# Attention stage: where the score maxima of later head groups stand between TensorE's other passes

## The chip, the cores and the metric

One Trainium2 chip, of which this kernel uses one core. The metric is the device time of one execution in microseconds (us), lower is better. A core has five engines that run their own instruction streams and wait for each other on semaphores: PE (TensorE, matmuls), DVE (VectorE), ACT (ScalarE), POOL (GpSimd) and SP (SyncE, here only a DMA queue). PE writes its results into eight PSUM banks, numbered 0 to 7, of 128 x 512 floats each.

## The reference

One macaron block over x of 2048 tokens by 512: half an expert layer, an attention, half an expert layer, each on a layernorm of x and added to x.

```python
x = x + 0.5 * _L0_ffn_ref(_layernorm(x), router_w, w1, w2, w3)
x = x + _L0_attn_ref(_layernorm(x), wq, wk, wv, wo)
x = x + 0.5 * _L0_ffn_ref(_layernorm(x), router_w, w1, w2, w3)
```

The attention is what the change touches. It has 16 query heads and 4 key and value heads of 32 columns, a rotary embedding on q and k, a causal mask and a softmax:

```python
attn = jnp.einsum('bhqd,bhkd->bhqk', q, k) / np.sqrt(HD)
attn = jnp.where(mask[None, None], -jnp.inf, attn)
attn = jax.nn.softmax(attn, axis=-1)
out = jnp.einsum('bhqk,bhkd->bhqd', attn, v)
return out.transpose(0, 2, 1, 3).reshape(b, t, d) @ wo
```

## The kernel before

The stages follow one another: routing and experts, the projections of q, k and v, attention, routing and experts again. All orders are written out by hand; each engine runs its own list.

In attention the work is cut into **groups** G = 0 to 15. Group G is the block b = G // 4 of 512 queries and the key head G % 4, with its four query heads. A group's **tiles** are (G, k), k = 0 to 4 b + 3, each 128 keys; the list `TILES` has 160 of them. For each tile PE makes four **scores** (L1614, one a head, keys on the partitions, 512 queries wide, fewer where the mask cuts), ACT takes exp of each (L1731, into P), POOL masks the diagonal tiles (L1770), and PE **weighs** V with them into bank 3 (L1626). Sums of P over the keys are made by PE with a matrix of ones into bank 4 (L1644) for tiles in `SUMMED`. From group 8 on, most tiles of a group are added up elsewhere instead: by POOL into CH (L1784, four additions a tile) and by DMAs that accumulate into CD (L1800), which PE sums once at the group's end (L1635). P has two buffers for groups 0 to 7, four after that.

Softmax needs a maximum over the keys for each query and head before the exp. It comes in as a bias: rows 96 and 97 of Qs hold the negative maximum (as a high and a low part) against ones in Ks, so the score already has it taken off. So for every group the maxima are made ahead of time, by a second set of products with the queries on the partitions: `pe_top` (L987) into a free bank, then `dve_top`, a reduction on DVE into a column of PM (L1000 where the mask doesn't cut, L1002 on the diagonal, which adds the mask and reduces). The page speaks of them as "bank<-Ks,Qs" and "PM<-bank". Such a maximum covers 512 keys, on the diagonal 128 to 512. `tops_of(G)` lists them: 16 times (b + 1) a group. Groups 0 to 3 get theirs during the projections, groups 4 to 15 during attention.

When a group's last maximum is through, `dve_found_in_bank` ("solvemax", L1033, L1038, L1040) brings PM together into M, PE transposes M ("found", L1049), ACT copies that to mT (L1058, "foundcopy"), and SP writes it to DRAM and reads it back into Qs (L1079, L1083). The group's first score waits for that.

`attend_plan` writes one list of steps, `g.plan`; every engine walks the same list and does the steps that are its own. For each tile n it appends four scores of tile n; after each score come the maxima that are due; after the second score one entry of `extra` (work of a finished block: its four out **projection** chunks "proj", L1681, then statistics, scaling, transposes and logits); after the fourth the weigh of tile n - 1, a solvemax ahead of it and a found behind it where one is due, and for a finished group "out", "tsum" (L1652) and "even" (L1661) at set distances. How many maxima are due follows from two counters, `weight` (work passed) and `given` (maxima put, a diagonal one by its share of 512 keys).

Maxima, projection chunks, tsum, even and found share a ring of banks, taken in turn: 5, 6 and 7, and 4 as well for a part of each group from 8 to 13. `pe_take` makes PE wait until the bank's last user, on DVE or ACT, has freed it. After the last maximum the scores get two of those banks in addition to their three (`g.wide`). PE runs its list in order, so a maximum that waits for a bank holds all that stands behind it.

Of the kernel before, what the change touches and what calls it, by code (L numbers as in the profile page):

```python
# [15 lines left out]
NB = 4  # L16
BQ = 512
# [959 lines left out]
def tops_of(G):  # L977
    return [("top", G, h, c, k) for h in range(4) for c in range(4) for k in range(G // 4 + 1)]
# [438 lines left out]
def first(b, k):  # L1417
    return max(0, k - 4 * b) * P


TILES = [(G, k) for G in range(4 * NB) for k in range(4 * (G // 4) + 4)]
# [20 lines left out]
def summed_by_pe(G):  # L1442
    others = added_by_pool(G) + added_by_dma(G) + added_by_dve(G)
    return [k for k in range(4 * (G // 4) + 4) if k not in others]


def numbered(tiles):
    return {n: i for i, n in enumerate(tiles)}
# [7 lines left out]
SUMMED = numbered(n for n, (G, k) in enumerate(TILES) if k in summed_by_pe(G))  # L1456
# [25 lines left out]
    return todo + [[("logits", b)], [("best", b)]]  # L1482


def attend_plan(g):

    ring, plan = g.ring, []
    ahead = [key for G in range(4, 4 * NB) for key in tops_of(G)]
    later = {}
    told, weight, given, extra, known, copying, free = 4, 0.0, 0.0, [], [], [], True  # L1490

    def put(at, step):
        later.setdefault(at, []).append(step)
# [7 lines left out]
    for n, (G, k) in enumerate(TILES):  # L1501
        b = G // 4
        for j in range(4):
            at = 4 * n + j
            plan.append(("score", n, j))
            weight += (BQ - first(b, k)) / BQ
            while ahead and given < 1.1 * weight:
                key = ahead.pop(0)
                given += 1 if key[4] < key[1] // 4 else (key[3] + 1) / 4
                plan.append(key)  # L1510
                if not ahead or ahead[0][1] != key[1]:
                    known.append((at + 1, key[1]))
                    told += 1
# [3 lines left out]
            if copying:  # L1517
                plan.append(("foundcopy", copying.pop()))
            if j == 1 and extra:
                plan += extra.pop(0)  # L1520
            if j == 3 and n:
                if known and known[0][0] <= at and free and n - 1 not in LAST.values():
# [5 lines left out]
                if n - 1 in LAST.values():  # L1528
# [5 lines left out]
                    if G0 % 4 == 3:  # L1534
                        if b == 1:
                            residual(at + 2, 0)
                        until = at + (34 if b == 1 else 9)
# [432 lines left out]
def build(nc, d, out):  # L1970
    ctx = ExitStack()
    with ctx:
# [11 lines left out]
        project_plan(g)  # L1984
        g.projected = {bank: g.ring.uses[bank] for bank in (5, 6, 7)}
        attend_plan(g)
        g.routed = [None, None]
        pe, act, dve, pool, sp = nc.tensor, nc.scalar, nc.vector, nc.gpsimd, nc.sync
# [118 lines left out]
```

## Time and profile before

| | |
|---|---|
| time, median of 3 runs | 1305.88 us (1305.64 to 1311.02) |
| the profiled execution, its own time | 1308.35 us |
| its span on the core | 1307.1 us |
| PE busy, share of the span | 90% |
| DVE, ACT, POOL busy | 69%, 50%, 46% |
| attention, first score to the last | 425.8 to 1029 us |
| mean granted clock of PE over the span | 0.964 |

The span is what the profiler saw on the core; the profiled execution's time has some 1.2 us around it. Busy shares are means over stages with different limits, so the attention stage has to be read by itself: by stretches of a group each, and in the timeline. Matmuls overlap in the rows (a full score lasts 0.40 us, and the next starts some 0.24 us later), so it is the distance between starts that tells what one costs. "PEld" is the load of a matmul's weights, which runs beside the matmuls and waits before they do. An instruction's row may name in brackets the idle time of its engine before it and what ended that.

### The profile page before, as it was taken

What the parts mean: (1) busy time and instruction counts of PE and PEld (TensorE: products, weight loads), DVE (VectorE), ACT (ScalarE), POOL (GpSimd) and SP (SyncE); (2) the same over time, 40 slices, a digit from 0 to 9 for tenths busy, and PEclk for the clock granted to TensorE, in tenths of its full rate; (3) what the DMA queues carried; (4) which work ended last, traced back from release to release, by engine and by line L of the source; (5) the groups of instructions that cost most, each with busy time, mean ns of one, the idle gap of its engine ahead of it and who ended that gap; (6) DMA issues with size and microseconds to landing.
All of it is one profiled execution on the core that took longest, in us unless ns stands there. A gap on an engine that the chain in (4) does not pass through costs nothing.

```text
span 1307.1 us, 21775 instructions
## 1 busy us (share of the span) xinstructions
PE 1174.8 (90%) x7252; PEld 773.6 (59%) x7252; DVE 902.5 (69%) x2104; ACT 660.1 (50%) x1313; POOL 596.7 (46%) x495
## 2 busy tenths in 40 slices
PE   4589999949998999999999999999999958999996
PEld 3468888728776555445545455445544436777774
DVE  8867777759997566476677677577754675666664
ACT  2545555426555555255456566356567733444442
POOL 4644544314110111001436556455582463888886
PEclk9789999979999899999999999999999968999999
DMA  9823333356430123014445845556733452666665
GB/s 339 337 90 114 107 112 106 121 170 108 88 69 4 33 47 55 1 38 95 98 107 153 163 98 121 171 130 158 144 88 65 136 197 52 99 106 101 101 103 72
DMA packets 66971, 146.92 MB, mean 112 GB/s; under 512 B 8784, under 2 KB 28240, under 8 KB 62864
## 3 DMA queue, kind: packets, MB, share of 16 engines
q0 software_dynamic: 35184, 93.34, 33.9%
q1 hardware_dynamic: 31680, 52.19, 11.7%
q8 instruction: 62, 1.02, 0.3%
q14 instruction: 45, 0.37, 0.1%
HBM read 79.71 MB, written 33.55 MB: 87 GB/s over the span
## 4 chain that ended last, share of the span: by engine, by line
PE 61%; DVE 16%; DMA 10%; issue 5%; ACT 3%; POOL 3%; SPq 0%; POOLq 0%; DVEq 0%; ACTq 0%
PE bank L830 10%; PE bank L1614 10%; PE bank L1626 9%; PE bank L987 8%; PE bank L853 6%; DMA out<-Y,DI 4%; PE bank L1644 4%; PE bank L1681 3%; DMA XG<-xn,TK 3%; DVE bank L1002 2%; DVE PM L1000 2%; PE bank L812 2%; POOL out L780 2%; PE bank L725 2%; PE bank L1379 2%
## 5 line engine op out<-in xcount | busy, mean ns | idle before, releaser
L1731 ACT ACTIVATE P<-bank 128x512 f32<-128x512 f32 (+3 forms) x640 | 303.4, 536 | 260.2 <-PE bank L1614 253.6
L1000 DVE TENSOR_REDUCE PM<-bank 128x1 f32<-128x512 f32 x384 | 252.6, 685 | 82.8 <-PE bank L987 82.0
L1614 PE MATMUL bank<-Qs,Ks 98*128 98x512 f32 (+3 forms) x640 | 241.1, 407 | 5.2 <-ACT P L1731 2.8
L987 PE MATMUL bank<-Ks,Qs 96*128 96x512 f32 (+3 forms) x640 | 234.2, 386 | 10.8 <-DVE PM L1002 5.4
L1614 PEld LDWEIGHTS bank<-Qs,Ks 98*128 98x128 f32 x640 | 117.2, 190 | 131.4 <-issue 59.4
L1770 POOL TENSOR_SCALAR_AFFINE_SELECT P<-P 128x512 f32<-128x512 f32 x64 | 42.7, 675 | 287.2 <-ACT P L1731 287.2
L1002 DVE CUSTOM_DVE_ANT_0 bank<-bank,KB 128x128 f32<-128x128 f32 (+3 forms) x256 | 124.6, 498 | 54.8 <-PE bank L987 54.1
L987 PEld LDWEIGHTS bank<-Ks,Qs 96*128 96x128 f32 x640 | 121.8, 191 | 56.8 <-DVE PM L1000 17.2
L1626 PE MATMUL bank<-P,V 128*32 128x512 f32 (+3 forms) x1280 | 151.5, 545 | 3.6 <-POOL P L1770 3.6
L780 POOL DMA_INDIRECT out<-Y,DI x78 | 127.6, 1636 | 41.7 <-issue 32.0
L1784 POOL TENSOR_TENSOR CH<-CH,P 128x512 f32<-128x512 f32 x108 | 139.2, 1434 | 14.1 <-ACT P L1731 13.4
L941 DVE TENSOR_TENSOR DL<-W,DH 128x512 fp32r<-128x512 f32 x152 | 98.3, 689 | 41.4 <-ACT DH L902 41.4
L757 POOL DMA_INDIRECT XG<-xn,TK x78 | 93.5, 1199 | 52.2 <-DVE TK L688 18.0
L902 ACT CAST DH<-W 128x512 fp32r x152 | 86.7, 618 | 20.9 <-issue 20.9
L830 PE MATMUL bank<-WH,XH 128*128 x312 | 94.1, 424 | 2.2 <-ACT XH L882 1.5
L830 PE MATMUL bank<-WL,XH 128*128 x312 | 87.0, 401 | 0.2 <-DVE XL L923 0.2
L830 PE MATMUL bank<-WH,XL 128*128 x312 | 85.5, 395 | 0.0
L769 POOL DMA_INDIRECT y<-Y,DI x39 | 38.7, 993 | 97.1 <-DVE Y L951 97.1
L923 DVE TENSOR_TENSOR XL<-bank,XH 128x512 fp32r<-128x512 f32 x78 | 53.9, 691 | 35.6 <-ACT XH L882 35.6
L882 ACT CAST XH<-bank 128x512 fp32r<-128x512 f32 x78 | 45.8, 587 | 58.4 <-PE bank L812 55.6
L888 ACT ACTIVATE G<-bank 128x256 f32<-128x256 f32 x78 | 29.9, 384 | 86.1 <-PE bank L830 86.1
L830 PEld LDWEIGHTS bank<-WL,XH 128*128 128x128 f32 x312 | 59.6, 191 | 15.3 <-issue 0.9
(193 smaller groups left out, 1946.9 us busy)
## 6 DMA issues: line engine op xcount, KB each, us to landing
CD<-P POOLq DMA_DIRECT2D x17, 1024.0 KB, 7.4
xn<-XN SPq DMA_DIRECT2D x8, 1024.0 KB, 5.9
WR<-L_ffn_w POOLq DMA_DIRECT2D x16, 512.0 KB, 15.1
XO<-y POOLq DMA_DIRECT2D x8, 1024.0 KB, 9.4
WR<-L_ffn_w SPq DMA_DIRECT2D x16, 512.0 KB, 7.7
CD<-P SPq DMA_DIRECT2D x7, 1024.0 KB, 5.3
CD<-CH POOLq DMA_DIRECT2D x7, 1024.0 KB, 7.5
XA<-y POOLq DMA_DIRECT2D x24, 256.0 KB, 4.2
```

The lines of the kernel that those rows point to most:

```text
L757: pool.indirect_dma_start(out=x.XG[:, j % NG, :], out_offset=None, in_=g.xnd[f][:, :], in_offset=bass.IndirectOffsetOnAxis(ap=r.TK[:, j:j ...
L780: pool.indirect_dma_start(out=g.out.rearrange("t (h d) -> (t h) d", h=2), out_offset=bass.IndirectOffsetOnAxis(ap=r.DI2[:, h, j:j + 1], ax ...
L830: ins = pe.matmul(bk(g, 2 + j % 2), part[:, k * P:k * P + P], w[:, bass.ds(ev[j] * 2048 + k * 512, 512)], start=(n == 0 and k == 0), stop= ...
L902: act.copy(x.DH[:, k, :], W.W3[:, bass.ds(e * 1024 + k * 512, 512)]).then_inc(s("dh"), 1)
L941: ins = dve.tensor_tensor(x.DL[:, k, :], W.W3[:, bass.ds(e * 1024 + k * 512, 512)], DHf[:, k, :], ALU.subtract)
L987: pe.matmul(bk(g, bank)[:, 0:n], g.Qs[b][0:96, G % 4 * 4 + h, c * P:c * P + P], g.Ks[0:96, G % 4, k * BQ:k * BQ + n], start=True, stop=Tru ...
L1000: dve.tensor_reduce(dst, bk(g, bank)[:, 0:n], AX.X, ALU.max).then_inc(s(f"free{bank}"), 1)
L1002: dve.tensor_tensor_reduce(out=bk(g, bank)[:, 0:n], in0=bk(g, bank)[:, 0:n], in1=g.KB[:, CB_MASK + BQ - n:CB_MASK + BQ], scale=1.0, scalar ...
L1614: pe.matmul(bk(g, bank)[:, o:BQ], g.Ks[0:98, G % 4, k * P:k * P + P], g.Qs[G // 4][0:98, G % 4 * 4 + j, o:BQ], start=True, stop=True).then ...
L1626: ins = pe.matmul(bk(g, 3)[32 * h:32 * h + 32, o:BQ], g.V[:, k, q * HD:q * HD + HD], a.P4[buffer_of(n)][:, h, o:BQ], start=(k == 0), stop= ...
L1731: act.activation(a.P4[buffer_of(n)][:, j, o:BQ], bk(g, score_bank(g, i))[:, o:BQ], ACT.Exp, scale=scale).then_inc(s("exp"), 1)
L1784: ins = pool.tensor_tensor(to[:, h, :], two[:, h, :], one[:, h, :], ALU.add)
```

## The change

Only `attend_plan` is touched, and two small functions that it calls are new. The pace at which maxima are put was 1.1 for each full score; the scores alone counted as passed work. Now `passes_of(n)` counts for a tile its scores, weighing and, in `SUMMED`, its sums, cut to the columns that the mask leaves, and one more; a projection chunk counts `PROJ_PASSES`. The share of maxima for each pass is set so that they come out even up to tile (14, 10), the eleventh of group 14. A projection's passes are added when its chunk is put, so its maxima come after the next score.

```diff
+PROJ_PASSES = 10
+
+def passes_of(n):
+    G, k = TILES[n]
+    return (8 + (4 if n in SUMMED else 0)) * (BQ - first(G // 4, k)) / BQ + 1
+
+def part_of(key):
+    return 1 if key[4] < key[1] // 4 else (key[3] + 1) / 4
...
+    until = TILES.index((14, 10))
+    share = sum(part_of(key) for key in ahead) / (sum(passes_of(n) for n in range(until)) + 3 * NB * PROJ_PASSES)
...
-            weight += (BQ - first(b, k)) / BQ
-            while ahead and given < 1.1 * weight:
+            weight += passes_of(n) / 4
+            while ahead and given < share * weight:
                 key = ahead.pop(0)
-                given += 1 if key[4] < key[1] // 4 else (key[3] + 1) / 4
+                given += part_of(key)
                 plan.append(key)
...
             if j == 1 and extra:
+                weight += PROJ_PASSES if extra[0][0][0] == "proj" else 0
                 plan += extra.pop(0)
```

All lines behind the new functions stand 20 lower in the new file (L1614 is L1634 there, L1626 L1646, L1644 L1664, L1681 L1701); L987 and L1049 stay.

The first place is PE at the second projection chunk of block 0, in tile (5, 3). Before, from the chunk to the weigh:

```order
L1681 MATMUL bank<-WO,OT_154 128x512 x4
L1614 MATMUL bank<-Qs_134,Ks 128x512
L987 MATMUL bank<-Ks,Qs_134 128x384
L987 MATMUL bank<-Ks,Qs_134 128x512
L1614 MATMUL bank<-Qs_134,Ks 128x512
L987 MATMUL bank<-Ks,Qs_134 128x512
L1626 MATMUL bank<-P_152,V 32x512 x4
```

And now, on PE at the same chunk:

```order
L1701 MATMUL bank<-WO,OT_154 128x512 x4
L1634 MATMUL bank<-Qs_134,Ks 128x512
L987 MATMUL bank<-Ks,Qs_134 128x256
L987 MATMUL bank<-Ks,Qs_134 128x512
L987 MATMUL bank<-Ks,Qs_134 128x384
L987 MATMUL bank<-Ks,Qs_134 128x512 x2
L987 MATMUL bank<-Ks,Qs_135 128x512
L1634 MATMUL bank<-Qs_134,Ks 128x512
L987 MATMUL bank<-Ks,Qs_135 128x512
L1646 MATMUL bank<-P_152,V 32x512 x4
```

Six maxima stand behind the chunk's score where there were two, in a ring of three banks (the second row of "x2" is the last diagonal one of a group, which is 512 wide too).

The second place is PE at find 13. Before, in tile (12, 10):

```order
L1614 MATMUL bank<-Qs_136,Ks 128x512
L987 MATMUL bank<-Ks,Qs_136 128x512
L1614 MATMUL bank<-Qs_136,Ks 128x512
L987 MATMUL bank<-Ks,Qs_136 128x128
L987 MATMUL bank<-Ks,Qs_136 128x512
L1626 MATMUL bank<-P_153,V 32x512 x4
L1049 MATMUL bank<-K,M_54 8x128 x4
```

And now, on PE in tile (12, 6):

```order
L1701 MATMUL bank<-WO,OT_154 128x512 x4
L1634 MATMUL bank<-Qs_136,Ks 128x512
L987 MATMUL bank<-Ks,Qs_136 128x512 x4
L1634 MATMUL bank<-Qs_136,Ks 128x512
L987 MATMUL bank<-Ks,Qs_136 128x512
L1646 MATMUL bank<-P_153,V 32x512 x4
L1049 MATMUL bank<-K,M_54 8x128 x4
```

The find has moved four tiles ahead, behind the last chunk of block 2 and five maxima. On DVE it stands behind the chunk's addition and the same five reductions.

## Rows read from the trace of the kernel before

**Rows 1.** The page's busy time of each engine.

```profile
PE 1174.8 (90%) x7252; PEld 773.6 (59%) x7252; DVE 902.5 (69%) x2104; ACT 660.1 (50%) x1313; POOL 596.7 (46%) x495
```

**Rows 2.** Busy time by stretch, groups 5 and 9; columns in the first line.

```profile
core 0: us, PE busy (x) PEld busy (x) DVE busy (x) ACT busy (x) POOL busy (x), PEclk, DMA share, GB/s
...
515.10:560.60 45.50, 44.52 (x269) 22.07 (x267) 24.11 (x64) 16.23 (x36) 2.54 (x4) 1.00 0.09 16
...
684.60:731.50 46.90, 43.95 (x326) 24.55 (x327) 34.03 (x91) 26.93 (x55) 26.57 (x24) 1.00 0.62 149
```

**Rows 3.** Timeline of PE, tiles (10, 6) to (10, 9) and (15, 5): start, us.

```profile
751.10 0.50 PE L1614 MATMUL bank<-Qs,Ks 98*128 98x512 f32 x1
...
754.28 0.50 PE L1614 MATMUL bank<-Qs,Ks 98*128 98x512 f32 x1
...
762.42 1.06 PE L1626 MATMUL bank<-P,V 128*32 128x512 f32 x8
...
1005.78 1.20 PE L1614 MATMUL bank<-Qs,Ks 98*128 98x512 f32 x4
...
1007.90 1.19 PE L1614 MATMUL bank<-Qs,Ks 98*128 98x512 f32 x4
```

**Rows 4.** Waits of PE, 625 to 1000 us: total, times, longest.

```profile
PE bank L1049 <- DVE M L1040: 5.8, 7, 1.6
PE bank L1626 <- POOL P L1770: 2.6, 3, 1.2
```

**Rows 5.** Waits of PE's weight loads, 625 to 1000 us.

```profile
PEld bank L987 <- DVE PM L1000: 10.6, 36, 0.4
...
PEld bank L987 <- ACT mT L1058: 2.5, 6, 0.5
...
PEld bank L1614 <- ACT mT L1058: 1.3, 1, 1.3
```

**Rows 6.** Waits of PE's weight loads, 425 to 625 us.

```profile
PEld bank L987 <- DVE PM L1000: 6.7, 21, 0.5
...
PEld bank L987 <- ACT mT L1058: 3.9, 5, 1.0
```

**Rows 7.** Busy time by stretch of 4 us, columns as in rows 2.

```profile
860.00:864.00 4.00, 2.35 (x15) 0.91 (x14) 3.67 (x11) 1.33 (x3) 4.00 (x5) 1.00 0.64 131
864.00:868.00 4.00, 3.91 (x23) 2.09 (x20) 1.96 (x9) 3.29 (x6) 2.29 (x2) 1.00 0.66 135
868.00:872.00 4.00, 2.70 (x12) 1.05 (x14) 3.85 (x13) 3.99 (x7) 0.00 (x0) 0.93 0.69 266
872.00:876.00 4.00, 4.00 (x22) 1.45 (x15) 1.56 (x3) 0.74 (x3) 1.43 (x2) 0.64 0.48 98
```

**Rows 8.** Timeline behind a projection chunk, tile (8, 3).

```profile
641.29 0.69 DVE L1833 TENSOR_TENSOR XO<-bank,XO 128x512 f32<-128x512 f32 x1 [2.26 <-PE bank L1681]
641.33 0.40 PE L987 MATMUL bank<-Ks,Qs 96*128 96x512 f32 x1
```

**Rows 9.** Timeline of maxima and a find, tiles (6, 0) and (6, 1).

```profile
558.01 0.57 DVE L1002 CUSTOM_DVE_ANT_0 bank<-bank,KB 128x384 f32<-128x384 f32 x1 [0.73 <-PE bank L987]
...
558.50 0.69 DVE L1000 TENSOR_REDUCE PM<-bank 128x1 f32<-128x512 f32 x1
...
560.31 1.27 DVE L1000 TENSOR_REDUCE PM<-bank 128x1 f32<-128x512 f32 x2
...
561.04 0.50 PE L987 MATMUL bank<-Ks,Qs 96*128 96x512 f32 x1 [0.24 <-DVE PM L1000]
...
565.20 0.16 DVE L1033 TENSOR_REDUCE bank<-PM 128x16 f32<-128x32 f32 x1
565.40 0.17 DVE L1038 CAST M<-bank 128x16 fp32r<-128x16 f32 x1
```

**Rows 10.** Timeline of POOL, tiles (10, 4) to (10, 8).

```profile
744.66 10.06 POOL L1784 TENSOR_TENSOR CH<-CH,P 128x512 f32<-128x512 f32 x8 [0.57 <-ACT P L1731]
...
755.56 5.01 POOL L1784 TENSOR_TENSOR CH<-CH,P 128x512 f32<-128x512 f32 x4
760.53 0.63 POOL L1770 TENSOR_SCALAR_AFFINE_SELECT P<-P 128x512 f32<-128x512 f32 x1
```

## The prediction

> **What bounds the kernel now.** I read the page first: PE is busy 1174.8 of 1307.1 us, DVE 902.5, POOL 596.7 [rows 1]. The change touches the attention stage alone, some 605 us of the span, so next came the busy time by stretch there: in groups 5 and 9 PE is busy 44.52 of 45.5 us and 43.95 of 46.9, at a granted clock of 1.00 [rows 2]. PE bounds the stage. A product for maxima ("a maximum" below) is PE work wherever it stands, so moving one gains nothing unless it takes a wait with it. I call a maximum over 512 keys one unit, a shorter one its share (128 keys a quarter).
>
> What a unit costs on PE comes from whole tiles in the timeline, from the first score of one to the first score of the next. Tile (10, 6) holds 4.5 units and takes 754.28 - 751.10 = 3.18 us; tile (15, 5) holds none and takes 1007.90 - 1005.78 = 2.12 [rows 3]. So a unit is (3.18 - 2.12) / 4.5 = 0.236 us, and neither tile has slack in it: at the density of before, a plain tile doesn't wait for DVE. I then looked at waits. From 625 us to 1000, PE sat idle 5.8 us in seven places before the transposes of "found" (L1049, for DVE's M) and 2.6 us for POOL's masks [rows 4]. Its weight loads, which run ahead and so wait longer than PE loses, waited 10.6 us for DVE to free the bank of a maximum and 2.5 + 1.3 us for the copy of mT on ACT [rows 5]; from 425 us to 625 the same two are 6.7 and 3.9 us [rows 6]. That is all the change can win: some 10 to 25 us of waits out of 1308.
>
> **The change, part by part.** Nothing is added or removed: 576 maxima of 504 units in all, 640 scores, 12 finds. What moves is where the maxima stand. The rate was 1.1 units a full score; it is now 504 / (1286 + 120) = 0.358 units a pass. A full tile without sums on PE counts 9 passes and gets 3.2 units instead of 4.4, one with sums counts 13 and gets 4.7, and a projection's chunk counts 10 and brings 3.6 at once. Counted over the plan, groups 0 to 4 change little (3.0 to 3.3 units a tile after 2.8, 3.9 after 3.5 in group 4), group 5 goes from 3.56 to 5.59, groups 9 to 11 and 13 from 3.8 to 3.9 down to 3.2, and the last maximum moves from (14, 7) to (14, 9).
>
> *Thinned tiles, a gain.* With 3 to 4 maxima a tile DVE keeps up. Of the 10.6 us of weight-load waits on DVE in the later stretch PE itself loses a part only; nothing shows which, so the bounds are 0 and 10.6, and I take 3.5, near the low end, because the plain tile of rows 3 has no wait and the waits sit where other DVE work (the inverse sums, statistics) comes between.
>
> *Finds, a gain.* "solvemax" stands behind the last maximum on DVE, and "found" behind one weigh on PE. In the later stretch the seven finds cost 5.8 us of idle PE [rows 4]. Six of the seven of after stand in tiles with less DVE work ahead or with a doubled weigh in front; I give them 1.2 us together. Find 13 is the exception: it moves from (12, 10) to (12, 6), right behind a projection's burst. DVE there has the projection's add and five maxima, 6 x 0.60 us, and the find's three short steps, 0.2 us apart [rows 9], 4.2 us in all, against PE's score, five maxima, score and weigh, 2.6 us: some 1.7 us of wait with the transfer of the last one. So 5.8 - 2.9 = 2.9 us gained, between 0 and 5.
>
> *The copy of mT, a gain.* A maximum that is next on the find's bank waits until ACT has copied it. With fewer maxima a tile the ring comes round later. Finds 6 and 8 to 14 no longer have a maximum on that bank within two or three scores, finds 4, 5 and 7 do. Of 3.9 + 2.5 + 1.3 us [rows 5, 6] I take 3, bounds 0 and 6.
>
> *A stretch at low clock, a gain.* From 860 to 872 us PE is busy 2.35, 3.91 and 2.70 of 4 us each, and from 872 to 876 the granted clock is 0.64 [rows 7], that is partly at the lower of its two levels, 1.2 GHz. The idle time is find 13 at (12, 10) and then a square root's table on ACT at (12, 11). The find goes from there, so the second wait stands alone, and I expect no fall: 4 us at 0.64 instead of 1.00 is 1.4 us, with the rest of a slow tile at its edges 2.0. Bounds 0 and 2.
>
> *Bursts behind projections, a loss.* Each of the 12 chunks (L1681) is followed in the new plan by a score and then 4 to 6 maxima in a row, where before stood 1 or 2. The ring has three banks in group 5, and DVE adds the chunk first. In the rows, with the first maximum at 641.33 as zero, DVE's add starts at -0.04 and lasts 0.69 [rows 8]. Two reductions in a row take 1.27 us, one of them 0.69, so the next instruction starts some 0.60 after a full one; a 384 wide one takes 0.57 and lets the next start after 0.49, and PE goes on 0.05 us after a reduction has ended (560.31 + 0.69 gives 561.00, PE 561.04) [rows 9]; for 256 columns I estimate 0.43 and 0.33 from these. At (5, 3) the row after the chunk is half, full, 3/4, full, full, full, score, full. PE starts them at 0, 0.12, 0.70 (chunk's bank, free at 0.65), 1.04, 1.63, 2.11, the score at 2.35, the last at 2.72, and ends at 2.96. Without waits it is 1.74: 1.2 us lost. Four such chunks in group 5 make 4.8; waits of 0.8 us that stood in these tiles already (they are in rows 6) come off: 4.0. With four banks (groups 8 and 12) the same working gives 0.3 to 0.5 for five in a row and 0 to 0.25 for four: 1.5 + 0.8 us for eight chunks. Together 6.3, bounds 2 (if reductions and the add overlap more than in these rows) and 9.
>
> *POOL, a loss.* POOL's additions don't get shorter when the maxima thin out. In group 10 eight of them start at 744.66 and take 10.06, four more at 755.56 take 5.01, the mask at 760.53 ends at 761.16, and PE's weigh needs it at 762.42 [rows 3, 10]. The stretch from 744.66 is 16.5 us of POOL and 17.8 of PE. PE loses 17.5 - 13.25 = 4.25 units there, 1.0 us, and the find's 0.7; it arrives after 16.1 and waits some 0.6 us. Groups 9 to 11 alike give 1.8, group 13 nearly reaches the same bound, say 0.4: 2.2 us, bounds 0 and 6. In group 14 the wait for the mask stays, since from (14, 4) POOL is the longer chain before and after.
>
> *Sum.* Gains 3.5 + 2.9 + 3.0 + 2.0 = 11.4; losses 6.3 + 2.2 = 8.5; net 2.9 us faster. The profiled execution took 1308.35 (span 1307.1), 2.5 above the median of 1305.88, so 1305.4 for it and **1303.0** for the median.
>
> **Rivals.**
> *Evenness pays in full.* If the waits for freed banks were PE's nearly whole, thinning gains 8 us instead of 3.5, mT 5 and the finds 4: 19 less 9.5, some 9.5 faster, **1296.5**. For it: the 36 waits of the later stretch sit in the very tiles that are thinned. Against it: the plain tile without slack [rows 3].
>
> *POOL takes over.* If POOL's chain from the second addition to the mask is the longer one in groups 9 to 13 more often than worked out, up to the bound of 6 us, what the thinning gives is handed to POOL: 2.9 - 3.8 = -0.9, **1306.8**. For it: 16.5 against 17.8 us, a slack of 1.3 that any gain eats. Against it: groups 8 and 12 stretch by the projections, and POOL has room there.
>
> *The bursts bring the clock down* (slower). In group 5 a burst lets PE idle 1.2 us in 2.96, four times 8 to 10 us apart, and find 13 idles 1.7 just behind another. If each of the five is followed by a stretch like 872 to 876, 2.0 us apiece, and the old fall stays, 2.9 - 10 - 2 makes 9 slower: **1312 to 1313**. [...] Against it: a tile of group 5 with 1.2 us of wait in some 9 is 87% busy, and group 9 with 2.95 us idle held 1.00 [rows 2]. The Trainium skill speaks for this rival ("TensorE: Matmul & The Clock Gate", section "A second HAM failure mode: psum-queue depth-cycling"): a kernel that cycled through PSUM banks let PE pause briefly between groups of matmuls, and its clock swung between the two levels. By that page the time would be this rival's 1312.5; the trace agrees in rows 7 and not in rows 2, so its chance stays small.
>
> **How the numbers follow.** The forecast 0.57 (1299.5 to 1307 by its bounds), evenness in full 0.21, POOL 0.13, clock 0.09. A measurement here tells about 0.5%, 6.5 us, from no change. Faster by more (below 1299.4): most of the second case and the low edge of the first, 0.24. Slower by more (above 1312.4): most of the clock's, 0.07. The rest, 0.69, is the same. For 8 in 10 the range leaves half of the second case below (0.11) and the clock's above (0.09): 1296 to 1310.
>
> **What would show it.** Right: in group 5 four gaps of some 1.2 us in maxima behind L1701, waiting for PM; groups 9 to 11 some 2 to 3 us shorter each and group 5 some 8 longer (2.03 units x 8 tiles x 0.236 = 3.8, and the waits); waits for M of some 3 us after 625 us; a granted clock of 1.00 at (12, 12); POOL's mask a little late in groups 10 and 11. Wrong: bursts without gaps, a second stretch of low clock, or thinned groups that don't shrink.

## The result and the profile after

The changed kernel takes **1319.41 us** (median of 5 runs, 1317.81 to 1323.43); the kernel before, beside it, 1306.71 (5 runs, 1305.64 to 1311.02). The ratio is **1.0093**, 95% interval 1.0069 to 1.0116: 12.7 us slower, where 1303.0 was forecast with a range of 1296 to 1310. The forecast has the wrong sign and the time lies outside the range. The profiled execution is the longest of the five, 1323.43 us with a span of 1322.2 (before 1307.1), so the places below add up to 15.1 us and not to 12.7.

The page's busy time of each engine, after, answers to [rows 1]:

```profile
PE 1182.8 (89%) x7252; PEld 774.5 (59%) x7252; DVE 907.8 (69%) x2104; ACT 657.9 (50%) x1313; POOL 597.2 (45%) x495
```

The counts are the same, as they must be. PE is 8 us longer at the same work: matmuls that ran at a lower clock, or stalled on their way. The rest is idle time.

To find the places I took the time from each group's first exp to the next group's. A unit of maxima that moves takes its 0.236 us of PE along, so the table's fifth column takes that off: what is left is what the move cost or gave.

| groups | before, us | after, us | units moved in | difference less 0.236 a unit | what the prediction had put there |
|---|---|---|---|---|---|
| 0 to 3 | 54.6 | 55.7 | 4.8 | 0.0 | 0 |
| 4 | 31.2 | 33.6 | 2.8 | +1.8 | 0 |
| 5 | 45.6 | 54.7 | 16.2 | **+5.3** | +4.0, bursts |
| 6 | 32.8 | 37.6 | 2.0 | **+4.3** | 0 |
| 7 | 34.8 | 34.5 | 2.8 | -0.9 | 0 |
| 8 | 55.6 | 60.6 | 5.8 | **+3.6** | +1.5, bursts |
| 9 to 11 | 129.5 | 119.9 | -24.5 | -3.9 | +1.8 POOL, and most of -3.5, -2.9, -3.0 |
| 12 | 73.7 | 76.0 | 2.5 | **+1.7** | +0.8 bursts, -2.0 clock |
| 13 | 58.0 | 57.5 | -11.2 | **+2.1** | +0.4 POOL |
| 14, 15 | 86.3 | 84.2 | -1.0 | -1.9 | 0 |

With +1.3 ahead of the attention and +1.8 behind it, where nothing was changed, that is the 15.1 us between the two spans. In one place the table shows this one execution more than the plan: group 9 takes 43.2 us here and 41.5 to 41.6 in the six variants below whose plan is the same there, so groups 9 to 11 gave nearer 5.5 us than 3.9.

Groups 5 and 9 in the busy time by stretch (columns as in [rows 2], the bounds by first exp):

```profile
517.07:571.75 54.68, 52.30 (x286) 25.07 (x285) 34.05 (x87) 16.77 (x35) 2.54 (x4) 1.00 0.15 37
704.44:747.67 43.23, 42.75 (x316) 23.93 (x317) 30.16 (x80) 26.36 (x57) 27.24 (x25) 0.96 0.65 158
```

Against [rows 2], PE's idle time in group 5 grew from 1.0 to 2.4 us and in group 9 it fell from 3.0 to 0.5. Note that "busy" hides part of group 5's loss: a matmul that stalls on its way is shown longer.

The waits that the prediction counted, after, answering to [rows 4 and 5] (638 to 1013 us) and, the last two, to [rows 6] (425 to 638):

```profile
PEld bank L987 <- DVE PM L1000: 3.2, 10, 0.4
...
PE bank L1634 <- ACT P L1751: 6.6, 3, 3.6
PE bank L1049 <- DVE M L1040: 4.5, 5, 1.7
```

```profile
PEld bank L987 <- DVE PM L1000: 11.6, 36, 0.7
...
PE bank L1681 <- DVE PM L1000: 2.6, 2, 2.4
```

The weight loads' waits for freed banks did fall in the thinned groups, from 10.6 us to 3.2. In the early groups they rose, from 6.7 to 11.6: there the ring has three banks and the maxima stand closer. And there are two waits that nobody had asked for: 6.6 us for P, one of them 3.6 long (before, 2.6 us in two places), and 2.4 us at L1681.

**Where the new waits stand.** The attention's first 12 us run partly at the lower clock in both kernels (0.93, 0.50 and 0.68 from 424 us before; 0.73, 0.70 and 0.50 after). From 440 us on, one stretch of 4 us before showed a clock well below 1.00 [rows 7]. After, seven do, at four places (columns as in [rows 2]):

```profile
584.00:588.00 4.00, 2.55 (x44) 1.55 (x48) 2.68 (x8) 1.97 (x3) 0.00 (x0) 0.82 0.01 4
588.00:592.00 4.00, 4.00 (x20) 1.63 (x12) 1.40 (x4) 1.63 (x3) 0.00 (x0) 0.75 0.00 0
704.00:708.00 4.00, 3.56 (x25) 1.81 (x29) 2.79 (x6) 3.04 (x8) 0.64 (x1) 0.76 0.00 2
708.00:712.00 4.00, 4.00 (x32) 2.45 (x23) 2.58 (x8) 2.76 (x5) 0.00 (x0) 0.82 0.66 262
884.00:888.00 4.00, 1.59 (x5) 1.37 (x6) 3.53 (x14) 3.67 (x7) 0.17 (x1) 0.87 0.16 33
888.00:892.00 4.00, 4.00 (x22) 1.32 (x21) 2.19 (x4) 1.07 (x2) 1.43 (x2) 0.70 0.16 33
948.00:952.00 4.00, 3.34 (x14) 1.10 (x18) 0.69 (x1) 1.75 (x4) 1.48 (x2) 0.57 0.62 127
```

Three of the four places are at a **solve**: the step in `finish_plan` in which DVE and ACT work out a finished block's layernorm scale (L294 to L318 on DVE, a square root on ACT at L338, with a load of ACT's table before it and another one back to exp). It is on neither engine's list of busy lines, since its steps are short. But both run in order, so a solve holds their lists up for some 2 us: maxima wait on DVE, exps on ACT.

*Tile (6, 2), block 0's solve.* Timelines of PE and DVE:

```profile
582.57 0.50 PE L987 MATMUL bank<-Ks,Qs 96*128 96x512 f32 x1
585.45 1.08 PE L1681 MATMUL bank<-K,R 128*32 128x128 f32 x32 [2.38 <-DVE PM L1000]
586.32 1.74 PE L1646 MATMUL bank<-P,V 128*32 128x512 f32 x8
587.77 2.00 PE L1664 MATMUL bank<-P,ones 128*32 128x512 f32 x8
```

```profile
582.84 0.17 DVE L297 TENSOR_SCALAR sm<-mv 128x4 f32<-128x4 f32 x1
583.61 0.18 DVE L310 RECIPROCAL sm<-sm 128x4 f32<-128x4 f32 x1 [0.60 <-ACT sm L338]
...
584.62 0.69 DVE L1000 TENSOR_REDUCE PM<-bank 128x1 f32<-128x512 f32 x1
```

PE stands at "even" (L1681), whose bank is held by a maximum that DVE reads only at 584.62, behind the solve. PE idles 2.38 us. Then the same weigh and sums that take 1.06 and 1.04 us elsewhere take 1.74 and 2.00: PE has been granted its lower level (1.2 GHz) for a while. In the kernel before, "even" stood in the same tile and found its bank free:

```profile
569.35 1.08 PE L1661 MATMUL bank<-K,R 128*32 128x128 f32 x32
```

*Tiles (12, 11) and (12, 12), block 2's solve.* DVE, POOL, ACT and PE:

```profile
881.29 2.91 DVE L297 TENSOR_SCALAR sm<-mv 128x4 f32<-128x4 f32 x1
```

```profile
878.94 5.22 POOL L1804 TENSOR_TENSOR CH<-CH,P 128x512 f32<-128x512 f32 x4
```

```profile
884.24 0.20 ACT L338 ACTIVATE sm<-sm 128x4 f32<-128x4 f32 x1 [2.41 <-DVE sm L297]
```

```profile
886.40 0.50 PE L1634 MATMUL bank<-Qs,Ks 98*128 98x512 f32 x1 [3.56 <-ACT P L1751]
```

An instruction on 128 x 4 numbers, 0.17 us in the solve of (6, 2), lasts 2.91 here. It ends at 884.20; POOL's run of four additions ends at 884.16. In the kernel before, the same instruction started 0.22 us behind the end of POOL's additions, and PE's wait was 1.30 us:

```profile
861.04 5.25 POOL L1784 TENSOR_TENSOR CH<-CH,P 128x512 f32<-128x512 f32 x4
```

```profile
866.51 0.17 DVE L297 TENSOR_SCALAR sm<-mv 128x4 f32<-128x4 f32 x1
```

```profile
869.68 0.50 PE L1614 MATMUL bank<-Qs,Ks 98*128 98x512 f32 x1 [1.30 <-ACT P L1731]
```

In the changed kernel ACT waits for it, with sqrt's table already loaded, the next exps wait behind that on ACT, and PE idles 3.56 us.

*Tile (13, 13).* ACT, POOL and PE:

```profile
948.11 1.76 ACT L1751 ACTIVATE P<-bank 128x384 f32<-128x384 f32 x4 [4.09 <-DMA CD<-P]
```

```profile
938.36 2.08 POOL L1820 DMA_DIRECT2D CD<-P  x1
```

```profile
948.66 0.69 PE L1634 MATMUL bank<-Qs,Ks 98*128 98x384 f32 x1 [1.82 <-ACT P L1751]
```

An exp here may overwrite P only when a transfer that POOL issues behind its additions has read it. POOL issued it at 938.36, behind the additions and a load of the residual, the exps began at 948.11, when it had landed, and PE idled 1.82 us.

The fourth place, at 704 us, is block 1's solve, with a wait of 1.18 us for P.

### The profile page after: what moved, and what is told of

It reads as the page before. It is cut to its first block, busy times and chain, and to the rows that moved or that the text cites. A ratio compares the mean times of both kernels' runs of the same rounds, so it can differ in the third digit from the quotient of the medians.

```text
span 1322.2 us, 21775 instructions
## 1 busy us (share of the span) xinstructions
PE 1182.8 (89%) x7252; PEld 774.5 (59%) x7252; DVE 907.8 (69%) x2104; ACT 657.9 (50%) x1313; POOL 597.2 (45%) x495
## 4 chain that ended last, share of the span: by engine, by line
PE 58%; DVE 17%; DMA 9%; POOL 6%; issue 6%; ACT 2%; SPq 0%; POOLq 0%; DVEq 0%; ACTq 0%
PE bank L830 10%; PE bank L1634 9%; PE bank L1646 8%; PE bank L987 8%; PE bank L853 5%; DMA out<-Y,DI 4%; PE bank L1664 4%; PE bank L1701 3%; POOL out L780 3%; DVE PM L1000 2%; DMA XG<-xn,TK 2%; DVE bank L1002 2%; POOL CH L1804 2%; PE bank L812 2%; PE bank L1379 2%
## 5 line engine op out<-in xcount | busy, mean ns | idle before, releaser
L1634 PE MATMUL bank<-Qs,Ks 98*128 98x512 f32 (+3 forms) x640 | 239.4, 408 | 8.4 <-ACT P L1751 6.6
L987 PE MATMUL bank<-Ks,Qs 96*128 96x512 f32 (+3 forms) x640 | 235.4, 390 | 10.9 <-DVE PM L1002 5.7
L1634 PEld LDWEIGHTS bank<-Qs,Ks 98*128 98x128 f32 x640 | 117.7, 191 | 137.3 <-ACT P L1751 68.3
L1646 PE MATMUL bank<-P,V 128*32 128x512 f32 (+3 forms) x1280 | 153.0, 550 | 3.5 <-POOL P L1790 3.5
L987 PEld LDWEIGHTS bank<-Ks,Qs 96*128 96x128 f32 x640 | 122.1, 192 | 56.4 <-DVE PM L1000 14.8
L1664 PE MATMUL bank<-P,ones 128*32 128x512 f32 (+3 forms) x664 | 68.3, 482 | 1.0 <-DVE PM L1000 0.5
```

Source lines behind the costliest of these rows:

```text
L987: pe.matmul(bk(g, bank)[:, 0:n], g.Qs[b][0:96, G % 4 * 4 + h, c * P:c * P + P], g.Ks[0:96, G % 4, k * BQ:k * BQ + n], start=True, stop=Tru ...
L1634: pe.matmul(bk(g, bank)[:, o:BQ], g.Ks[0:98, G % 4, k * P:k * P + P], g.Qs[G // 4][0:98, G % 4 * 4 + j, o:BQ], start=True, stop=True).then ...
L1646: ins = pe.matmul(bk(g, 3)[32 * h:32 * h + 32, o:BQ], g.V[:, k, q * HD:q * HD + HD], a.P4[buffer_of(n)][:, h, o:BQ], start=(k == 0), stop= ...
L1664: ins = pe.matmul(bk(g, 4)[32 * h:32 * h + 32, o:BQ], g.ones[:], a.P4[buffer_of(n)][:, h, o:BQ], start=fresh, stop=last)
```

## The experiments

Each edit is against the changed kernel unless another is named. The kernel before was measured beside them (medians 1306.4 to 1307.8 us), and each ratio is to that. Two questions: is the loss the bursts behind projection chunks, and is it what the moved maxima meet elsewhere?

### No counting of the chunks

```diff
-PROJ_PASSES = 10
+PROJ_PASSES = 0
```

> The changed kernel with PROJ_PASSES 0: a projection chunk brings no maxima of its own, the other passes carry them all (0.392 units a pass instead of 0.358). Theory A (bursts behind the 12 chunks cost some 7 us, and waits that collide with the square roots and with POOL, each followed by a stretch at low clock, cost the rest): the gaps behind L1701 in group 5 go, group 5 falls from 54.7 us to some 46 (2.7 of it are units that move elsewhere), and the time is 1308 to 1313. Rival B (the thinned groups 9 to 13 make POOL and its DMAs the bound, bursts matter little): groups 9 to 13 have 3.5 units a tile here instead of 3.2, so little changes there, 1316 to 1320. Rival C (bursts are the whole loss): 1303 to 1307, at or below the kernel before.

1311.66 us (1306.13 to 1314.51), ratio 1.0027 [1.0009, 1.0046]. Group 5 falls from 54.7 to 47.5 us at 34 units for 45, group 8 from 60.6 to 56.1, group 6 only to 36.9. L1681 at (6, 2) still waits 2.58 us, though here no low clock follows, and low clock stays at two other solves, of blocks 1 and 2. Counting the chunks costs some 8 us, more than half of the loss, and not all of it. Not all of the 8 us are bursts: the edit moves maxima in every group, and in group 12 (72.1 us for 76.0, with 9.5 units fewer) L297 takes 0.98 us instead of 2.91.

### The same number of maxima, spread

```diff
-            weight += passes_of(n) / 4
+            weight += passes_of(n) / 4 + (owed.pop(0) if owed else 0)
...
-                weight += PROJ_PASSES if extra[0][0][0] == "proj" else 0
+                owed += [PROJ_PASSES / 4] * 4 if extra[0][0][0] == "proj" else []
```

> The changed kernel, but a chunk's 10 passes are counted over the four scores that follow it, 2.5 each, so the same tiles have nearly the same number of maxima and no four to six stand in a row. Theory A: the 12 gaps go (6 to 8 us less in groups 5, 8 and 12) and find 13 waits less; where solves and POOL's chain fall stays nearly the same, so their waits stay: 1311 to 1314. Rival B: 1317 to 1320. Rival C: 1305 to 1308.

1312.15 us (1309.13 to 1313.29), ratio 1.0031 [1.0017, 1.0044]. Seven us less, but not where I looked: group 5 stays at 54.0 us (54.7) and groups 8 and 6 fall by 0.9 and 0.2. What falls is group 12 (73.0 for 76.0), where L297 takes only 0.86 us, group 13 (55.8 for 57.5) and group 9 (41.5 for 43.2, as in the other variants); the low clock at block 1's solve and at (13, 13) is gone. So group 5's loss is not the row of maxima behind a chunk as such; it comes with their number.

### Block 2's solve one place later

```diff
+    todo += [[("rest", b)]] if b == 2 else []
     todo += [[("store", b), ("solve", b)]]
```

"rest" is a step that no engine does; the store, the solve and all that stands behind them in `extra` come four scores later.

> The changed kernel with the finish of block 2 held back by one tile between its statistics and its solve. In the changed kernel DVE's 128x4 addition of the solve (L297) lasts 2.91 us beside an addition of POOL at (12, 11) and ends with it, PE then idles 3.56 us and 888 to 892 us run at 0.70. Theory A: L297 takes 0.17 us again if no addition of POOL runs then, PE's wait before (12, 12) or (12, 13) falls to some 1.3 us, the low stretch goes: 3 to 5 us less, 1314.5 to 1316.5. Rival: the wait is ACT's two table loads and comes with the solve wherever it stands: no change, 1319.

1311.20 us (1308.28 to 1317.95), ratio 1.0039 [1.0016, 1.0062]. Group 12 takes 71.4 us for 76.0, group 13 55.0 for 57.5; L297 takes its 0.17, 0.6 us behind the end of POOL's additions. The move gives 7 to 8 us back, more than the 3 to 5 that were expected: the wait at (13, 13) went with it, and PE has none above 1 us in group 13.

### Block 0's solve one place later

```diff
+    todo += [[("rest", b)]] if b == 0 else []
     todo += [[("store", b), ("solve", b)]]
```

> The changed kernel with the finish of block 0 held back by one tile between its statistics and its solve. In the changed kernel the step even(5) in tile (6, 2) takes the bank of a maximum that stands behind the solve on DVE, PE idles 2.38 us and 584 to 592 us run at 0.82 and 0.75. Theory A: with the solve in tile (6, 3) even(5) no longer waits, tile (6, 2) falls from 9.3 us to some 5.5 and the low stretch goes: 3 to 4 us less, 1315.5 to 1316.5. Rival: the wait comes back one tile later in the maxima behind the solve: 1318 to 1320.

1314.54 us (1312.44 to 1316.65), ratio 1.0058 [1.0039, 1.0077]. Group 6 takes 33.9 us for 37.6, group 7 35.4 for 34.5; group 12 stays at 77.2, and L297 there is held again:

```profile
873.48 2.93 DVE L297 TENSOR_SCALAR sm<-mv 128x4 f32<-128x4 f32 x1
```

```profile
871.13 5.24 POOL L1805 TENSOR_TENSOR CH<-CH,P 128x512 f32<-128x512 f32 x4
```

It ends at 876.41, POOL at 876.37.

### Block 2's solve without its first step

```diff
+    late = R.f == 1 and k == 2
...
+    if late:
+        return
     dve.wait_ge(dv.sem, dv.n)
     dve.tensor_scalar(sm[:, 0, c0:c1], R.mv[:, c0:c1, 1], 1e-5, None, ALU.add).then_inc(s(f"var{R.f}"), 1)
...
+    if R.f == 1 and k == 2:
+        parts[0] = R.mv[:, c0:c1, 1]
...
+    src = R.mv[:, c0:c1, 1] if R.f == 1 and k == 2 else R.sm[:, 0, c0:c1]
```

For block 2 the kernel leaves out the addition of 1e-5; square root and Newton's steps read the variance itself.

> The changed kernel with the addition of 1e-5 (L297) left out of block 2's solve alone, its square root and Newton step taken from the variance itself; the solve stays where it is. Theory (DVE's L297 was held 2.9 us by an addition of POOL, and ACT's square root and with it the exps of tile (12, 11) and (12, 12) waited for it): PE's wait there falls from 3.56 us to between 1 and 1.8, the low stretch behind it shrinks or goes: group 12 3 to 4 us shorter, 1315 to 1317. A later step of the Newton iteration may be held in its place, which ACT does not wait for. Rival (the later solve of the run before won by moving other work of block 2, L297 is beside the point): group 12 as in the changed kernel, 76 us, 1319.

1317.01 us (1312.29 to 1321.32), ratio 1.0074 [1.0048, 1.0101]. No gain that can be told, and the reason is in the rows: the next instruction of that kind is held in its place.

```profile
881.78 0.18 DVE L320 RECIPROCAL sm<-sm 128x4 f32<-128x4 f32 x1 [0.82 <-ACT sm L349]
881.99 1.91 DVE L322 TENSOR_TENSOR sm<-sm 128x4 f32<-128x4 f32 x1
883.93 0.16 DVE L324 TENSOR_TENSOR sm<-sm,mv 128x4 f32<-128x4 f32 x1
```

```profile
878.64 5.23 POOL L1815 TENSOR_TENSOR CH<-CH,P 128x512 f32<-128x512 f32 x4
```

The reciprocal, with POOL at work, takes its 0.18; the product of two small tensors takes 1.91 and ends at 883.90, POOL at 883.87. So it isn't that one line, and leaving an instruction out doesn't help as long as POOL adds. PE's waits there fall from 3.56 to 1.93 us, but the clock is at 0.62 and 0.53 in the two stretches from 884, and group 12 takes 76.4 us, as the rival had it. So that L297 is held is in the rows; what it costs is not shown by leaving it out, only by the moved solve.

### Both solves later

```diff
+    todo += [[("rest", b)]] if b in (0, 2) else []
     todo += [[("store", b), ("solve", b)]]
```

> The changed kernel with both solves, of block 0 and of block 2, one tile late. If the two runs with one each removed waits of their own, the gains add: after late solve 2 (ratio 1.0039) and late solve 0 (1.0058) of the changed kernel's 1.0093 the ratio is 1.0093 - 0.0054 - 0.0035 = 1.0004, 1307. If part of both was chance of the low stretches, it is 1.003 to 1.004, 1311.

1309.36 us (1304.49 to 1312.98), ratio 1.0027 [1.0004, 1.0051]: 10 us of the 12.7 are gone with every maximum in its changed place; the time lies between the two that were expected. At (6, 2):

```profile
583.70 1.08 PE L1682 MATMUL bank<-K,R 128*32 128x128 f32 x32 [0.19 <-DVE PM L1000]
584.57 1.07 PE L1647 MATMUL bank<-P,V 128*32 128x512 f32 x8
585.43 1.07 PE L1665 MATMUL bank<-P,ones 128*32 128x512 f32 x8
```

The wait is 0.19 for 2.38, and weigh and sums are back at 1.07 us each. From the tile's first score to the next one it is 5.55 us (580.88 to 586.43) for 9.26 (580.44 to 589.70): 3.7, of which 2.2 is the wait and 1.6 the clock behind it. From 440 us on, no stretch of 4 us in the attention has a clock below 0.99. The plan is still 0.27% slower than the kernel before: moving the solves takes the collisions away and leaves the rest of the loss.

### POOL's queue in group 13

```diff
-        put(at + 22, ("xoy", b, 1))
+        put(at + (22 if b < 3 else 46), ("xoy", b, 1))
```

> The changed kernel with the second accumulating load of block 3's residual (L1837, issued by POOL in tile (13, 8)) moved 24 scores later. In the changed kernel the exps of (13, 13) wait until the DMA CD<-P of tile (13, 9), issued at 938.36 behind POOL's additions and two such loads, has landed at 948.1; PE idles 1.82 us and 948 to 952 us run at 0.57. Theory (POOL's list and its DMAs are the longer chain in group 13): the issue comes some 1 us earlier and lands faster, the wait and the low stretch go, group 13 falls from 57.5 us to some 55: 2 to 3 us less, 1316.5 to 1317.5. Rival (the additions alone set it): less than 1 us, 1318.5 to 1319.5.

1315.25 us (1312.90 to 1319.50), ratio 1.0074 [1.0053, 1.0095]. Group 13 takes 54.1 us for 57.5, and the exp no longer waits for the transfer (the column's idle time before it is 1.90 us, ended by PE). POOL's queue does bind in group 13, by that transfer and not by the mask as the prediction had it.

### Maxima inside a chunk

```diff
...
+            if k < 3 and inner:
+                pe_top(g, inner.pop(0))
```

Up to two of the maxima that a chunk brings go between its four products, where DVE idles (2.98 us at (5, 3)).

> The changed kernel, but up to two of the maxima that a projection's chunk brings stand between its four matmuls instead of behind it. Theory (DVE idles during a chunk's 3.4 us and cannot make up for it behind it, which is why counting the passes over four scores did not shorten group 5): DVE gets 1.2 us of work inside each chunk, group 5 falls from 54.7 us to 50 or 51, groups 8 and 12 lose 0.5 to 1.5 each: 4 to 6 us less, 1313 to 1315. Rival (a maximum costs the same wherever it stands near a chunk, group 5 is long for another reason): 1318 to 1320.

1318.56 us (1314.70 to 1320.12), ratio 1.0073 [1.0049, 1.0098]. No gain: group 5 takes 56.8 us for 54.7. The chunk itself now waits, since its bank is the next one in the ring:

```profile
533.91 0.51 PE L987 MATMUL bank<-Ks,Qs 96*128 96x128 f32 x2
535.43 1.13 PE L1709 MATMUL bank<-WO,OT 128*128 128x512 f32 x2 [1.01 <-DVE PM L1000]
```

From the last maximum ahead of the chunk to the weigh behind it are 7.87 us (533.91 to 541.78) for 7.65 without (536.49 to 544.14).

### The kernel before, both solves later

The edit of "Both solves later", made in the kernel before.

> The kernel before, with one edit: the solves of blocks 0 and 2 are issued one place (of four scores) later than their stores. It asks whether moving the solves speeds up any plan or only mends the collisions that the change made. Theory A (the collisions are of the change's making: the kernel before has one stretch of low clock in the attention, at 872 to 876, and no 2.91 us instruction on DVE): within 0.2% of before, at most 2 us less, 1304 to 1308. Theory B (the solves cost either plan the same): some 8 to 10 us less than before, 1297 to 1299.

1307.09 us (1302.75 to 1312.05), ratio 0.9993 [0.9975, 1.0011]. The stretch of [rows 7] is at 1.00 and group 12 takes 72.5 us for 73.7, no more: PE now waits 1.92 us at the sums in tile (12, 12) (L1645), whose bank is held by a maximum behind the moved solve. The collisions that cost 10 us are the change's own.

### No counting, and both solves later

> The changed kernel with PROJ_PASSES at 0 (chunks of projections do not count, so nothing is made up for behind them) and with the solves of blocks 0 and 2 one place later. Theory A (the loss is the sum of two things, the maxima made up for behind chunks, some 8 us, and two solves that DVE and POOL hold up, some 10 us): the two edits add as far as they meet different places: PROJ_PASSES 0 alone gave 1311.7 with low clock left at the solves of groups 5, 9 and 12, so this one gives 1303 to 1307, without a stretch of low clock in the groups 5 to 13. Theory B (the two edits cure the same loss): 1309 to 1312, as each alone.

1305.21 us (1301.68 to 1308.31), ratio 0.9988 [0.9967, 1.0008]. The two causes add, less what they share: 7.8 and 10.0 us alone, 14.2 together. That is the whole loss; the time can't be told from the kernel before. Beside "Both solves later" (1.0027) it says what counting the chunks costs with the collisions away: 0.39%, 4 to 5 us. Group 12 takes 67.6 us. From 440 us on, low clock is left at one place, block 1's solve:

```profile
692.14 1.02 PE L1049 MATMUL bank<-K,M 128*8 128x128 f32 x4 [2.84 <-DVE M L1040]
```

### The same, and POOL's queue in group 13

> As the run before it, and the load of the second half of block 3's residual is issued 46 scores behind the first step of its kind and not 22, so that POOL's issues in group 13 stand ahead of it. Theory A (the landing of a carried sum behind POOL's queue costs group 13 up to 3 us, as the lines at 948 of the changed kernel show): 1 to 3 us less than the run before it, 1301 to 1305, if group 13 still waits there. Theory B (group 13 is only late because of what came in with group 12, and moving the solve already mends it): within 1 us of the run before it.

1305.16 us (1303.37 to 1308.25), ratio 0.9992 [0.9978, 1.0007]: nothing on top. Group 13 takes 56.2 us for 56.3. What it had to mend was already mended.

### Evenness by itself

In the kernel before: groups 9 to 13 keep their number of maxima, and only within a group are they put by passes.

```diff
+            fair = (BQ - first(b, k)) / BQ
+            if 9 <= G <= 13:
+                mates = [m for m in range(len(TILES)) if TILES[m][0] == G]
+                rate = 4 * sum((BQ - first(b, TILES[m][1])) / BQ for m in mates) / sum(passes_of(m) for m in mates)
+                fair = rate * passes_of(n) / 4
-            weight += (BQ - first(b, k)) / BQ
+            weight += fair
```

> The kernel before with the evenness alone: in groups 9 to 13 the maxima are paced by the tile's own passes (9 or 13), but each group keeps the number that it has in the kernel before, and chunks do not count. It takes the prediction's first gain by itself. Theory A (tiles whose sums stand beside maxima as dense as elsewhere leave TensorE waiting for DVE; the prediction's 3.5 us): 2 to 5 us less than before, 1302 to 1305. Theory B (groups 9 to 11 of the changed kernel are shorter only because their maxima were moved to groups 4, 5 and 8): within 1.5 us of before.

1308.14 us (1303.71 to 1311.26), ratio 1.0009 [0.9988, 1.0030]. By the time alone evenness is worth nothing that can be told. By the rows it isn't so: groups 9 to 11 take 127.5 us for 129.5, and group 12 takes 75.8 for 73.7, because find 13 has come to stand behind block 2's solve, and that beside POOL's additions (L297 at 860.37 for 1.99 us; POOL's end at 862.32):

```profile
865.74 1.02 PE L1049 MATMUL bank<-K,M 128*8 128x128 f32 x4 [4.74 <-DVE M L1040]
```

### Evenness by itself, both solves later

> The run e12_within (evenness alone in groups 9 to 13) with the solves of blocks 0 and 2 one place later, to be read beside e9_before_late (the kernel before with the same move, 1307.09). In e12_within the solve of block 2 was held beside POOL's additions (its first step took 1.99 us) and the find of group 13 stood right behind it, so that group 12 lost 2.1 us that have nothing to do with evenness. Theory A (evenness is worth what groups 9 to 11 showed, 2.0 us): 1303.5 to 1306, and group 12 at about 72 us. Theory B (evenness is worth nothing, the 2.0 us come back elsewhere): 1306 to 1309. The prediction's own term was 3.5 us.

**1302.17 us** (1298.58 to 1304.40), ratio **0.9961** [0.9944, 0.9978]. Faster than both kernels, by 5.6 us and 17. Beside the kernel before with the same move of the solves (0.9993) evenness is worth 0.3%, some 4 us, with intervals of 0.17% on either. The profiled execution, 1298.58 us, is the shortest of the ten, and the attention's first 12 us ran at 1.00 in it. Its stretches show 0.5 us in groups 9 to 11 (129.0 for 129.5), 1.8 in group 12 (70.7 for 72.5) and 0.4 in group 13. In group 9 two stretches of 4 us ran at 0.75 and 0.83; without them, as in the run before this one, the group is 1.5 us shorter (45.0 for 46.6). So I count 3 to 4. PE's wait at the sums behind the moved solve stays (1.96 us for the 1.92 there).

### No counting, all three solves later

> The run e10_no_burst_late (1305.21) with the solve of block 1 one place later as well. There the find of group 9 stands right behind that solve: TensorE waits 2.84 us for M, and two stretches behind it have a granted clock of 0.50 and 0.72. Theory A (a find or a maximum behind a solve costs its wait and some 2 to 3 us of low clock behind it): 3 to 5 us less than that run, 1300 to 1303, no low clock in the attention, and faster than the kernel before by 0.2 to 0.5%. Theory B (the wait is only moved to the next place): within 1.5 us of 1305.

1303.84 us (1296.58 to 1308.54), ratio 0.9968 [0.9949, 0.9987]. Group 8, which held the wait, takes 52.5 us for 55.4, and the find waits 0.32 for 2.84:

```profile
688.42 0.60 PE L1049 MATMUL bank<-K,M 128*8 128x128 f32 x4 [0.32 <-DVE M L1040]
```

The wait is gone and the group's share is as expected (3 to 5 us); in the medians it is 1.4, and the two intervals overlap. Low clock isn't gone from the attention, as was expected: behind find 15, where PE waits 0.55 and 0.92 us, the stretch from 972 us is at 0.59. It is faster than the kernel before, and not to be told from the run ahead of it.

## Why the prediction was wrong

*What bounds the kernel: right.* PE bounds the stage, a unit costs 0.236 us, and the waits named were real.

*Thinned tiles, 3.5 us: the size fits.* Evenness alone, once nothing else stood in its way, was worth 3 to 4 us, though nearly half of it in group 12, which the term didn't name. The waits of [rows 5] fell from 10.6 us to 3.2. In the changed kernel groups 9 to 11 together gave 3.9 beyond the units that left them, nearer 5.5 without the low clock at 704 us, which is this term, finds, mT and POOL in one; no run takes the term by itself with the groups' changed numbers.

*Finds, 2.9 us: half right.* 5.8 us became 4.5, not 2.9. Find 13, reckoned at 1.7 us, waited 1.47. Find 10 alone waited 1.68, where the six others had been given 1.2 together.

*Copy of mT, 3.0 us:* in weight loads 7.7 us [rows 5, 6] became 5.6; how much of the 2.1 PE felt isn't shown.

*Bursts, a loss of 6.3 us: right in kind, too small.* The worked example held: 2.96 us were worked out from the first maximum behind the chunk at (5, 3) to the end, and it is 3.16 from that maximum to the start of the weigh behind it.

```profile
537.20 3.70 PE L1701 MATMUL bank<-WO,OT 128*128 128x512 f32 x8 [0.20 <-DVE PM L1000]
540.34 0.80 PE L1634 MATMUL bank<-Qs,Ks 98*128 98x512 f32 x1
540.98 0.51 PE L987 MATMUL bank<-Ks,Qs 96*128 96x256 f32 x2
541.69 1.97 PE L987 MATMUL bank<-Ks,Qs 96*128 96x384 f32 x4 [0.20 <-DVE XO L1853]
...
544.14 1.06 PE L1646 MATMUL bank<-P,V 128*32 128x512 f32 x8
```

Group 5 lost 5.3 for 4.0 and group 8 3.6 for 1.5. For group 12 no run takes it by itself: with both solves later it takes 71.4 us in the changed plan and 72.5 in that of before, of which 1.9 are the wait at the sums. What I took for a matter of place is, in group 5, one of number: 16.2 units more made it 9.1 us longer, 0.56 us each, which is near DVE's 0.60 a maximum and far from PE's 0.236. Spreading them and putting them into the chunk left that as it was. It isn't a fixed price: without the counting, 5.5 units more cost group 5 1.9 us, 0.35 each, and the other 10.8 units cost 7.2, 0.67 each. That DVE's time is what sets it fits these numbers and isn't shown by a run of its own; DVE is busy 34.05 of the group's 54.68 us, and idle during a chunk (2.98 us at (5, 3)).

*The stretch at low clock, a gain of 2.0: wrong, and this is the step that failed.* It says "The find goes from there, so the second wait stands alone, and I expect no fall". The second wait is block 2's solve, and it was taken over at its old length. In the new plan that solve stood beside POOL's additions, PE waited 3.56 us instead of the 1.30 of the kernel before, and the two stretches behind were granted 0.87 and 0.70; group 12 lost 1.7 us where 2.0 of gain and 0.8 of bursts were put. More widely, the prediction asked of each moved maximum what it waits for, and never what the solves, which were not moved, would now find: at (6, 2) a bank, at (12, 11) POOL, and at block 1's solve a find or the next exps. With the two solves four scores later 10 us came back, and the same move in the kernel before gave nothing. That is the larger part of the 16.4 us between the forecast and the time, and not the whole: with the solves moved the change is still 0.27% slower, some 3.5 us, where 2.9 us of gain were forecast. The bursts (8.9 us in groups 5 and 8 for 5.5) and group 4 (1.8 for 0) account for most of that.

*POOL, a loss of 2.2: right in size, wrong in place.* PE's waits for masks stayed at 2.5 us (2.6 in [rows 4]), so groups 9 to 11 lost nothing there; group 13 lost 2.1 us for 0.4, by a transfer in POOL's queue. Moving a load out of its way gave group 13 3.4 us. The working had a slip as well: an arrival at 16.1 us against a POOL stretch of 16.5 is a wait of 0.4 us a group, not 0.6.

*The rivals.* "The bursts bring the clock down" had the sign and the second half of the mechanism: an idle PE, then a slow one. Its places were wrong. Group 5 with its four bursts was granted 1.00 throughout; the clock fell behind waits of 1.2 to 3.6 us at solves and at (13, 13). Its time was added up wrongly too: 9 us slower than the kernel before is 1315, not 1312 to 1313, which takes the 2.9 us of gain off twice. The rule of the Trainium skill cited there ("TensorE: Matmul & The Clock Gate", section "A second HAM failure mode: psum-queue depth-cycling") tells of a PE that pauses briefly and often between groups of matmuls and swings between its levels. The bursts it was cited for are nearest to that, and in group 5 the trace doesn't agree (1.00); at the four places one longer wait stands before each fall, of 2.38, 1.18, 3.56 and 1.82 us. "Evenness pays in full" would have been 6.5 us better than the forecast; evenness paid about what the forecast had. Its own sum takes off losses of 9.5 us, where the terms above have 8.5, and no reason is given.

*The range.* Its upper end, 1310, took in the bursts' bound (9 for 6.3) and POOL's rival, 1306.8, and left the clock rival above it. No term stood for a collision with a step that isn't moved, and that was worth more than any of the others.

What stays open: why group 4 lost 1.8 us with only 2.8 units more (its weight loads wait more for DVE, as in group 5, but nothing was run for it), and the place at 704 us, block 1's solve, whose low clock the changed kernel shows in its profile and seven of its variants (the runs on spreading, on the three moves of solves, on L297, on POOL's queue and on maxima inside a chunk) don't, with the same wait of 1.18 or 1.19 us.

## What to carry to other kernels

When steps are moved in an order that several engines walk, look up every short step that stays and that makes one engine wait for another (here a 128 x 4 layernorm solve with two table loads): its price is set by what stands behind it, and the move changes that. Ask which engine is last where a moved step goes to, and don't price it only by the one that bounds the stage as a whole. And when an idea seems to bring nothing, look in the trace whether it was paid back in a collision: moving two solves, with what stands behind them, by four scores turned no difference into 0.4% faster.

## What the runs showed of the hardware

Small DVE instructions with all operands in SBUF were held by POOL's additions, to the end of a run of four. L297 (128 x 4, 0.17 us) took 2.91 us in the changed kernel, and in six other runs above 0.98, 0.86, 2.93, 2.92, 2.92 and 1.99; L322, a product, took 1.91. In all eight the instruction ended 0.03 to 0.05 us behind POOL's last addition, though the four additions start only some 1.24 us apart and the record of one spans some 1.5. Reductions from a PSUM bank beside the same additions, and the reciprocal (0.18 us), were not held:

```profile
879.01 1.97 DVE L1000 TENSOR_REDUCE PM<-bank 128x1 f32<-128x512 f32 x3
```

The Trainium skill ("SBUF — State Buffer", section "Who interferes with whom") has the rule: a tensor_scalar in a two-port mode, or a tensor_tensor with both inputs in SBUF, and a GpSimd instruction that reads SBUF want the same pair of ports (the tensor_tensor its read half), and the second one waits until the first has finished. The traces agree on which instructions are held. They differ on how long: as I read the page, a wait should end with the addition that is running, some 1.5 us at most by its record, and in six of the eight it lasted through the next ones too, up to 2.9 us.

The other surprise is the price of a wait. At (6, 2) PE idled 2.4 us, and the clock behind it cost 1.6 more. It isn't certain each time: with the chunks not counted the same place waited 2.58 us and the clock stayed at 1.00, as it did behind the 1.92 us in the kernel before with its solves moved.
